# Null keys of a wide attention: their weights turned once per sequence, and who adds each head's projection to the residual

## What is computed

```
nkv = null_kv.reshape(HEADS, NUM_NULL_KV, 2, DIM_HEAD)
nk = broadcast(nkv[:, :, 0]); nv = broadcast(nkv[:, :, 1])
k = concatenate([nk, k], axis=2)
v = concatenate([nv, v], axis=2)
q = _l2norm(q) * q_scale
k = _l2norm(k) * k_scale
sim = einsum('bhid,bhjd->bhij', q, k) * ATTN_SCALE
sim = sim + dist * slopes
sim = where(causal_mask, neg, sim)
attn = softmax(sim, axis=-1)
out = einsum('bhij,bhjd->bhid', attn, v)
return out.transpose(0, 2, 1, 3).reshape(b, n, HEADS * DIM_HEAD) @ w_out
...
x = x + _L0_attn_ref(_layernorm(x, axis=-1), ...)
```

## Time and profile before

| | |
|---|---|
| Median of 3 runs | 2622.32 us (2617.93 to 2629.57) |
| Profiled execution | 2621.87 us, span of its instructions 2620.2 us |
| TensorE matmuls busy | 2392.0 us, 91% of the span |
| VectorE busy | 1722.9 us, 66% |
| ScalarE busy | 1481.1 us, 57% |
| GpSimd busy | 1605.7 us, 61% |
| Stage 0 | from the first statistics at 27.6 us to the last projection at 834 us |
| L891, additions to XR (stages 0 and 4) | 512 instructions, 376.2 us busy, 735 ns each |
| L770, products into T (stages 0 and 4) | 256 instructions, 163.8 us, 681 ns each |

### The profile page before, as it was taken

The page is one execution under the profiler, slowest core; times in us unless marked ns, Lnnn a source line. Parts: engine busy times, 40 slices in busy tenths (PEclk is TensorE's granted clock), DMA queues, the critical chain, the costliest instruction groups (busy, mean ns, idle before and its releaser), DMA issues. The chain is left out here.

```text
span 2620.2 us, 62757 instructions
## 1 busy us (share of the span) xinstructions
PE 2392.0 (91%) x24121; PEld 1873.6 (72%) x24121; DVE 1722.9 (66%) x4520; ACT 1481.1 (57%) x3071; POOL 1605.7 (61%) x2517
## 2 busy tenths in 40 slices
PE   4999999999998778888999999999999958789897
PEld 3888888888887556556777787787777748555555
DVE  4667677677775657785544467777777622477776
ACT  3666666666654457765444366666666523366665
POOL 4777777778786644443433267777777721566664
PEclk8999999999999969999999999999999979799999
DMA  3692000000000010000000000000000036000000
GB/s 115 205 331 84 2 2 2 2 2 2 2 2 1 1 53 2 2 2 1 23 1 1 3 2 6 6 4 6 6 6 4 6 116 190 17 8 10 8 4 33
DMA packets 23257, 83.12 MB, mean 32 GB/s; under 512 B 4113, under 2 KB 11026, under 8 KB 21938
## 3 DMA queue, kind: packets, MB, share of 16 engines
q1 hardware_dynamic: 19810, 71.90, 8.5%
q0 software_dynamic: 3152, 7.21, 0.9%
HBM read 71.89 MB, written 46.79 MB: 45 GB/s over the span
## 5 line engine op out<-in xcount | busy, mean ns | idle before, releaser
L891 POOL TENSOR_TENSOR XR<-XR,T 128x256 f32<-128x256 f32 x512 | 376.2, 735 | 151.9 <-DVE T L770 121.7
L645 ACT ACTIVATE P<-ps 128x384 f32<-128x384 f32 (+1 forms) x512 | 250.6, 542 | 177.4 <-PE ps L2575 176.0
L2575 PE MATMUL ps<-P,V 128*64 128x256 f32 (+3 forms) x4096 | 334.6, 348 | 7.0 <-DVE O L1396 5.2
L1380 DVE TENSOR_REDUCE bm<-ps 128x3 f32<-128x384 f32 x512 | 260.1, 550 | 100.5 <-PE ps L2575 99.8
L2575 PEld LDWEIGHTS ps<-P,V 128*64 128x64 f32 (+1 forms) x4096 | 186.3, 124 | 126.7 <-issue 32.2
L1305 ACT ACTIVATE P<-ps 128x768 f32<-128x768 f32 x256 | 207.7, 811 | 101.9 <-PE ps L2575 99.7
L781 DVE TENSOR_REDUCE sm<-ps 128x2 f32<-128x512 f32 (+1 forms) x256 | 130.8, 553 | 179.1 <-PE ps L2575 178.9
L1480 POOL TENSOR_SCALAR_AFFINE_SELECT P<-P 128x512 f32<-128x512 f32 x256 | 162.6, 635 | 124.3 <-ACT P L1305 122.4
L904 POOL TENSOR_TENSOR PS<-P 128x256 f32<-128x256 f32 x256 | 181.5, 734 | 69.5 <-ACT P L645 69.1
L2575 PE MATMUL ps<-mk,identb 128*128 128x256 bf16 (+1 forms) x1024 | 205.5, 296 | 17.2 <-DVE bm L1380 15.4
L912 POOL TENSOR_TENSOR ss<-ss,nhalf 128x16 f32<-128x16 f32 x64 | 187.8, 2934 | 5.3
(11 more groups left out here) (323 smaller groups left out, 7152.0 us busy)
## 6 DMA issues: line engine op xcount, KB each, us to landing
rows_i<-in_zero SPq DMA_DIRECT2D x16, 1208.0 KB, 32.0
rows_o<-in_zero SPq DMA_DIRECT2D x16, 1208.0 KB, 81.6
w<-in_m_w SPq DMA_DIRECT2D x23, 578.0 KB, 4.0
zt<-rows_i SPq DMA_DIRECT2D x23, 128.0 KB, 3.1
rows_o<-yo POOLq DMA_DIRECT2D x23, 128.0 KB, 3.7
stg<-in_t_w SPq DMA_DIRECT2D x11, 256.0 KB, 2.7
XR<-in_x SPq DMA_DIRECT2D x4, 512.0 KB, 8.4
out<-XR SPq DMA_DIRECT2D x8, 256.0 KB, 2.0
```

What stands on the lines that cost most here:

```text
L645: e.activation(self.P[at % 6][:, :], K.ps.ap("st", s, g, h)[:, 0:self.w], ACT.Exp, bias=0.0, scale=1.0 if kind == 0 else 0.125).then_inc(K ...
L891: p = po.e.tensor_tensor(x, x, self.T[g % 2][:, par, pr], ALU.add)
L1380: e.tensor_reduce(bm[:, h, :], K.ps.ap("mx", s, g, h)[:, 0:384].rearrange("p (a c) -> p a c", c=128), X, ALU.max, negate=True).then_inc(K. ...
L2575: return self.te.matmul(o, l, r, start=start, stop=True, skip_group_check=True)
```

## The change

Null keys: their scores are made by GpSimd (`pool_null`), the sum of the two exponents joins the sum of the others on VectorE just before the reciprocal, and GpSimd multiplies the exponents by the reciprocal into `pn` (`shared`), now [128 tokens, 64] for a whole sequence, in plain fp32 without a low part. Once per sequence a new item `null` of three steps, from tick 16b + 43, turns `pn` on TensorE, copies it on ScalarE, multiplies it by the projected null values `nvw` into a new bank `nul`, and VectorE adds that to the residual. `nvw` is made once from the null values and `wO`, in unit 0 at step 8 (`pe_nvw`, `act_nvw`). The matmuls of `pnT` leave `pe_pv`. Residual: `dve_sum` reads each 128x128 block of Y from PSUM, multiplies it by its reciprocal and adds it to XR, eight instructions a unit; `T` and GpSimd's additions are gone from stage 0. VectorE has an order of its own in which `prep` comes last in its tick. The end of a sequence (`done`) is the read of `nul`. The biases are loaded first, then the null values in one DMA in place of three. The core of the diff:

```diff
+            if kind == 0:
+                items.append((16 * b + first + 12 + unit, 2, "null", (b,), 3))
...
+        self.dve_order = [w for w in ticks(items, self.dve_rank) if not self.is_early(*w)]
...
     def done(self, b):
-        return self.summed, 4 * b + 4
+        return self.K.ps.read("nul", self.s, b) if self.kind == 0 else (self.summed, 4 * b + 4)
...
+        if name == "null":
+            return 3 if k == 0 else 2
...
+    def dve_rank(self, name, k):
+        return 6 if self.kind == 0 and name == "prep" else self.rank(name, k)
...
+    def pe_nvw(self, pe):
+        K, n = self.K, self.nvs_at
+        ps = K.ps.take(pe, self.G, "nvw")
+        K.staged(pe, n)
+        for j in range(8):
+            p = pe.e.matmul(ps[0:64, 0:128], K.stg[n % 2][:, 64 * j:64 * j + 64], K.wO[:, 128 * j:128 * j + 128],
+                            start=j == 0, stop=j == 7)
+        p.then_inc(K.ps.full_of("nvw"), 1)
+
+    def pe_null(self, pe, b, k):
+        K, s = self.K, self.s
+        if k == 0:
+            ps = K.ps.take(pe, self.G, "pnT", s, b)
+            pe.wait_ge(self.shared, 4 * b + 4)
+            K.tr(ps[0:64, 0:128], self.pn[b % 2][:, :]).then_inc(K.ps.full_of("pnT", s, b), 1)
+        if k == 1:
+            ps = K.ps.take(pe, self.G, "nul", s, b)
+            pe.wait_ge(self.nvs_in, 1)
+            pe.wait_ge(*K.ps.read("nvw"))
+            pe.wait_ge(*K.ps.read("pnT", s, b))
+            K.acc(ps[:, 0:256], self.pnT[b % 2][:, :], self.nvw[:, :], start=True).then_inc(K.ps.full_of("nul", s, b), 1)
...
-            if kind == 0:
-                pe.wait_ge(self.pnull, g + 1)
-                for i in range(2):
-                    p = K.tr(ps[0:96, 256 + 128 * i:384 + 128 * i], fv(self.pn[g % 2][:, i, :]))
...
-            for pr in range(2):
-                c = 256 * u + 128 * pr
-                K.acc(pv[:, 256 * pr:256 * pr + 256], self.nvs[:, 0, c:c + 128], self.pnT[g % 2][:, :], start=pr == 0)
-            K.acc(sm[:, 0:256], self.nvo[:, 4 * u:4 * u + 4, :].rearrange("p h c -> p (h c)"), self.pnT[g % 2][:, :],
-                  start=True)
...
+            elif name == "null":
+                if k == 2:
+                    b = a[0]
+                    xs = K.XR[:, 2 * b:2 * b + 2, :].rearrange("p t c -> p (t c)")
+                    dv.wait_ge(*K.ps.read("Y", self.s, 4 * b + 3, 1))
+                    dv.wait_ge(*K.ps.filled("nul", self.s, b))
+                    e.tensor_tensor(xs, K.ps.ap("nul", self.s, b)[:, 0:256], xs, ALU.add).then_inc(
+                        K.ps.out_of("nul", self.s, b), 1)
...
+            if kind == 0:
+                dv.after(dv.step(e.tensor_tensor(rs[:, :], sums, self.sm[g % 4][:, 48:56], ALU.add)))
+            e.reciprocal(rs[:, :], rs[:, :] if kind == 0 else sums).then_inc(K.ps.out_of("sT", s, g), 1)
...
+    def dve_sum(self, dv, b, g):
+        K, s, e, done = self.K, self.s, dv.e, [0, 0]
+        if g > 0:
+            dv.wait_ge(*K.ps.read("Y", s, g - 1, 1))
+        for par in range(2):
+            dv.wait_ge(*K.ps.filled("Y", s, g, par))
+            for pr in range(2):
+                for t in range(2):
+                    x, at = K.XR[:, 2 * b + t, :], 4 * t + 2 * pr + par
+                    if (par, pr, t) == (1, 0, 1):
+                        dv.wait_ge(*K.ps.read("Y", s, g, 0))
+                    elif par or pr:
+                        dv.after(done[t])
+                    i = e.scalar_tensor_tensor(x, K.ps.ap("Y", s, g, par)[:, 256 * pr + 128 * t:256 * pr + 128 * t + 128],
+                                               self.rs[g % 2][:, at:at + 1], x, ALU.mult, ALU.add)
+                    if pr == 1 and t == 1:
+                        i.then_inc(K.ps.out_of("Y", s, g, par), 1)
+                    else:
+                        done[t] = dv.step(i)
...
+    def pool_null(self, po, g):
...
+        po.after(po.step(e.tensor_tensor(sn, snr, rq, ALU.mult)))
+        e.tensor_tensor(sn, sn, nb, ALU.add).then_inc(self.scored, 1)
...
+            e.tensor_tensor(sm[:, 48:56], ex[:, :, 0], ex[:, :, 1], ALU.add).then_inc(self.pnull, 1)
+        if k == self.tk["out"]:
...
+            e.tensor_tensor(
+                self.pn[b % 2][:, :].rearrange("p (t h n) -> p t h n", t=2, n=2)[:, :, 4 * u:4 * u + 4, :], ex,
+                self.rs[g % 2][:, :].rearrange("p (t h) -> p t h", t=2).unsqueeze(3).to_broadcast([128, 2, 4, 2]),
+                ALU.mult).then_inc(self.shared, 1)
```

More of the change, by code:

```diff
@@ L171, in __init__ @@
         self.S = [sb(f"S{s}_{i}", [128, 256], F32) for i in range(2)]
-        self.T = [sb(f"T{s}_{i}", [128, 2, 2, 2, 128], F32) for i in range(2)]
+        if kind == 2:
+            self.T = [sb(f"T{s}_{i}", [128, 2, 2, 2, 128], F32) for i in range(2)]
         self.rs = [sb(f"rs{s}_{i}", [128, 8], F32) for i in range(2)]
@@ L182, in __init__ @@
             self.sn = [sb(f"sn{s}_{i}", [128, 64], F32) for i in range(2)]
[L183 to L186, removed]
+            self.pn = [sb(f"pn{s}_{i}", [128, 64], F32) for i in range(2)]
+            self.pnT = [sb(f"pnT{s}_{i}", [64, 128], F32) for i in range(2)]
+            self.nvw = sb(f"nvw{s}", [64, 256], F32)
             self.on = sb(f"on{s}", [128, 128], F32R)
@@ L502, in pe_pv @@
                     p = K.acc(pv[64 * par:64 * par + 64, 256 * pr + q:256 * pr + q + w], V[:, kt, 2 * pr + par, :],
[L503 removed]
+                              P[2 * pr + par][:, c:c + w], start=kt == 0 and pr == 0)
         p.then_inc(K.ps.full_of("pv", s, g), 1)
@@ L507, in pe_pv @@
                 for h in range(4):
-                    p = K.acc(sm[32 * h:32 * h + 32, q:q + w], self.one[:, 0:32], P[h][:, c:c + w])
+                    p = K.acc(sm[32 * h:32 * h + 32, q:q + w], self.one[:, 0:32], P[h][:, c:c + w], start=kt == 0)
             p.then_inc(K.ps.full_of("sm", s, g), 1)
@@ L545, in act @@
                 a[0].act(ac, a[1], k)
+            elif name == "null":
+                if k == 0:
+                    b = a[0]
+                    if b >= 2:
+                        ac.wait_ge(*self.K.ps.filled("nul", self.s, b - 2))
+                    ac.wait_ge(*self.K.ps.filled("pnT", self.s, b))
+                    ac.e.activation(self.pnT[b % 2][:, :], self.K.ps.ap("pnT", self.s, b)[0:64, 0:128], ACT.Copy).then_inc(
+                        self.K.ps.out_of("pnT", self.s, b), 1)
             elif name == "unit":
@@ L548, in act @@
                     self.act_kb(ac)
+                if self.kind == 0 and a == (0, 0) and k == 8:
+                    self.act_nvw(ac)
                 self.act_unit(ac, *a, k)
@@ L670, in dve @@
                 K.ps.out_of("beff"), 1)
-        for name, a, k in self.order:
+        for name, a, k in self.dve_order:
             if name == "prep":
@@ L820, in dve_null @@
-    def dve_null(self, dv, b, u):
-        K, s, g, e, ss, sm = self.K, self.s, 4 * b + u, dv.e, self.ss[(4 * b + u) % 4], self.sm[(4 * b + u) % 4]
-        rq = ss[:, 32:40].rearrange("p (t a r) -> p t r a", t=2, a=2).unsqueeze(4)
-        snr = self.sn[b % 2][:, :].rearrange("p (t h n) -> p t h n", t=2, n=2)[:, :, 4 * u:4 * u + 4, :].rearrange(
-            "p t (a r) n -> p t r a n", a=2)
-        sn = sm[:, 16:32].rearrange("p (t r a n) -> p t r a n", t=2, r=2, a=2)
-        nb = K.pc("nbias", 8 * u, 8).rearrange("p (a r n) -> p r a n", a=2, r=2)
-        dv.wait_ge(*K.ps.read("sn", s, b))
-        dv.wait_ge(self.unitq, 2 * g + 1)
-        if g >= 4:
-            dv.wait_ge(self.rec, g - 3)
-        for t in range(2):
-            d = dv.step(e.tensor_tensor(sn[:, t], snr[:, t], rq[:, t].to_broadcast([128, 2, 2, 2]), ALU.mult))
-        dv.after(d)
-        for t in range(2):
-            d = dv.step(e.tensor_tensor(sn[:, t], sn[:, t], nb, ALU.add))
-        dv.after(d)
+    def dve_null(self, dv, b, u):
+        g, e, sm = 4 * b + u, dv.e, self.sm[(4 * b + u) % 4]
+        dv.wait_ge(self.scored, g + 1)
@@ L867, in pool @@
                     self.pool_halves(po, 4 * a[0] + a[1], k - 1 - self.tk["st"])
-                if k == self.tk["out"] + (1 if self.kind == 2 else 0):
+                if self.kind == 2 and k == self.tk["out"] + 1:
                     self.pool_sum(po, *a)
@@ L935, in sp @@
         if self.kind == 0:
-            for n, (a, b) in enumerate(((0, 512), (512, 1024), (1024, 1040))):
-                n += self.nvs_at
-                K.sp_stage(sp, n, K.stg[n % 2][0:96, 0:b - a], K.t["nvs"][:, a:b])
             for c in range(5):
```

107 lines of the change are left out of this document (55 added, 52 removed).

## The result

The changed kernel takes 2641.54 us, the median of five runs (2637.66 to 2645.2), against 2622.32 before. The ratio is 1.0071, 95% interval 1.005 to 1.0092: slower by 19 us where 8 were forecast, inside the range. By the forecast's own bands (faster under 2609, slower over 2635) that is "slower", which had 0.38, and not "no change", which had 0.45. Its profiled execution took 2645.2 us, span 2643.5.

The account below looks back on a forecast made before the run. TensorE was taken to bound the first wide attention. Removed 51.4 us, added 59.7 (three bank waits included), net +8.3 on the profiled 2621.87 gave 2630.2, rounded up to 2631; range 2603 to 2660.

Parts of the forecast that it names:

- TensorE's matmuls and transposes: TensorE, each unit: two pn transposes and three pnT matmuls removed, 0.76 us, 48.6 us over 64 units.
- null transpose and product: TensorE, once per sequence: one added transpose and one fp32 matmul of 256 columns, 0.61 us, 9.8 us over 16.
- KL, tick 2: Unit with the next sequence's z and statistics: TensorE waits 1.35 us for KL's bank, 14 times, 18.9 us.
- bank of zT, tick 6: VectorE takes prep last, so v waits 0.60 us for the bank zT's low half frees, 14 times, 8.4 us.
- bank of nul, tick 14: Scores opening tick 14 wait for VectorE's null addition, behind two maxima and a reduction: 1.44 us, 15 times, 21.6 us.
- The sum step: VectorE, each unit: eight 128x128 steps, 0.26 us each, 2.08 in all, where T held 1.20.
- the first rival: VectorE's eight sum steps stand end to end, 0.34 us each, 2.72 in all: 2657 us; chance 0.16.
- second rival: The new TensorE waits bring clock falls to 0.50, ten times 1.5 us: 2646 us; chance 0.12.
- The end of the stage: Stage 1 waits for the last residual, which comes earlier without GpSimd's adds: gain 1.4 us.
- The case of the three waits: The forecast itself, with TensorE's waits for the KL, zT and nul banks: 2618 to 2642 us; chance 0.50.
- The regular unit's room of 0.11 us: Regular units: KL's bank is usable at 5.56 us, TensorE arrives at 5.67, so no wait.
- The rival "TensorE stays the bound": Bank waits lie elsewhere or VectorE is further ahead, so only TensorE's sum counts: 2581 us; chance 0.12.

Follow-up runs that it names:

- the kernel with the old residual: The changed kernel with T on VectorE and GpSimd's four additions back in stage 0, null keys as changed: 2664.86 us, ratio 1.0173 to the kernel before.
- the run: The changed kernel with GpSimd's early statistics for stage 1 (`ahead`) last in their tick: 2630.94 us, ratio 1.0045 to the kernel before.
- four ordering edits: The changed kernel with null addition first, early statistics last, z behind KL, and prep last except zT's low half: 2585.01 us, ratio 0.9863 to the kernel before.

## Why the prediction was right or wrong

The mechanism was right: TensorE's saving counts in full only where nothing is late, and three banks come back late once a sequence, at the three places and behind the three steps named. Each was taken away by itself and its price came back. The sizes, per sequence:

| Term, us per sequence | predicted | timeline after | by removing it |
|---|---|---|---|
| TensorE's matmuls and transposes | -3.04 | -2.36 | |
| its waits for pn | -0.10 | -0.10 | |
| null transpose and product | +0.61 | +0.83 | |
| KL, tick 2 | +1.35 | +1.13 | 1.14 |
| bank of zT, tick 6 | +0.60 | +0.37 | 0.41 |
| bank of nul, tick 14 | +1.44 | +1.39 | 1.33 |
| sum | +0.86 | +1.26 | drift +1.17 |

**The step that failed: the saving, 0.76 us a unit.** It was read as the distances of starts of the removed steps, 0.21 + 0.33 + 0.22. What stands in front of `P,V` changed too: 0.36 us from `raw` to `pnT,nvs` before, 0.53 from `raw` to `P,V` after. So 0.59 us is saved, and 64 x 0.17 = 10.9 us are missing. This also makes TensorE arrive later at the banks of KL and zT, and both waits are shorter than predicted. At zT's it arrives 4.84 us after R (508.26) in place of 4.69, and goes on 5.21 after R in place of 5.29. At KL's it arrives 5.84 after R (495.98 to 501.70, and 0.12) in place of 5.75. That is only 0.09 later, because the 5.75 had in it the 0.09 us by which KL held TensorE already. It goes on 6.98 after R in place of 7.10. So VectorE's side was right to 0.1 us in both.

**The null product.** 0.50 us was taken from `P,V`; the records give 527.65 - 526.81 - 0.12 = 0.72 us, where 0.12 is the pace of `wA,zT`. Its transpose lengthens the way from `nm` to `P,V` from 0.75 to 0.86 (522.31 to 523.17). Together 0.83: the product just above its upper bound of 0.7, and 3.5 us more over 16 sequences.

**The sum step was right.** 0.26 us a step and 2.06 in all, where 2.08 was forecast and 2.72 was the first rival's. The group of VectorE by shape, 0 to 830 us:

```profile
L849 DVE SCALAR_TENSOR_TENSOR XR<-ps,rs,XR 128x128 f32<-128x128 f32 x480 | 129.1, 343 | 0.0
...
L730 DVE TENSOR_TENSOR XR<-ps,XR 128x256 f32<-128x256 f32 x14 | 5.8, 415 | 0.0
```

One is 343 ns long and they start 0.26 apart, each waiting for the one before the last. By the rule of the Trainium skill (VectorE: DVE Perf Modes, "The DRAIN you can't avoid") they would stand end to end; this trace does not agree. The same section allows that an instruction which is not held starts earlier.

**The clock, second rival.** It did not come as priced. Through the 1.39 us at the null bank the granted clock stayed at full, the 2.4 GHz level:

```profile
530.00:532.00 2.00, 0.98 (x8) 0.74 (x7) 2.00 (x4) 1.32 (x3) 0.00 (x0) 1.00 0.00 0
532.00:534.00 2.00, 1.80 (x26) 1.59 (x28) 0.37 (x3) 0.10 (x1) 0.22 (x1) 1.00 0.00 0
```

It fell during the 4.18 us for `pn`, and, in the kernel with the old residual, during the 1.91 us for `raw`. The Trainium skill (TensorE: Matmul & The Clock Gate, "Part 1: The HAM clock gate") says that an idle TensorE is throttled back; both falls agree. The waits of 1.0 to 1.4 us, and 6 of the 14 waits of 1.9 us for `raw`, show that not every idle stretch brings one.

**What was missed: `pn` behind `ahead`.** The prediction went through VectorE's queue and the PSUM ring, and of GpSimd it said only that it gets "two small steps per unit" and, with ScalarE's, that "Neither is on the path". But `shared` is a new step on GpSimd that TensorE waits for. Its rank puts it behind the early statistics, once in the stage. Worth 6.0 us by the run. The kernel before had a gap of its own at this place, on its TensorE:

```profile
767.20 0.63 PE L2578 MATMUL ps<-ident,raw 128*128 128x128 f32 x4 [1.17 <-POOL raw L917]
...
768.59 0.47 PE L2578 MATMUL ps<-ident,pn 128*96 128x128 f32 x2 [0.54 <-POOL pn L928]
```

With it went a stretch of 3.4 us at half clock (768.8 to 772.2, part of it in the earlier trace rows), which costs half of that. So the net is 6.0 - (1.17 + 0.54 + 1.7) = 2.6 us.

**The end of the stage** gained 0.6 us, not 1.4: the time from the last `wO,OT` to the first statistics went from 6.47 us (833.27 to 839.74) to 5.92 (852.25 to 858.17), and VectorE's last addition starts at 855.73, 2 us ahead of a cast at 857.83 that waits for ScalarE and stands in front of those statistics. So the residual does not set that start.

The account over the stage: -64 x 0.59 - 1.4 + 16 x 0.83 + 14 x 1.13 + 14 x 0.37 + 15 x 1.39 + 2.6 - 0.6 = +18.0 us. Measured +18.4. The start of the stage is not in this sum. The one-time projection of the null values, put at 1 us in a start where TensorE was said to wait anyway, does not lie in that wait but behind it: 2.74 us from its start to the next matmul (47.58 to 50.32, changed kernel, most of it at half clock). What it costs in the end is not shown, since unit 7 comes only 0.76 us later than before, and runs differ by more than that there. So the agreement to 0.4 us is closer than the parts allow.

**How much of the number was luck.** 17.8 us were missing from the forecast (10.9 of the saving, 3.5 of the null product, 2.6 at `pn`, 0.8 at the end), and 7.1 too much was in it (3.1 for KL, 3.2 for zT, 0.8 for the null bank), so the errors cancel in part. The case of the three waits was given 2618 to 2642, and 2641.54 lies in it by half a microsecond.

**Not as the prediction said it would show.** The wait for the null bank is called "issue", not `<-DVE XR`. By the forecast's own test ("wrong if TensorE shows no waits for XR") I would have dropped a right theory; the gap in the starts of `mk,identb` was the row to name. GpSimd's busy time fell by 167 us (170 forecast). The drift makes the period 49.6 us where "about 49" was said. The regular unit's room of 0.11 us held: no wait shows there.

**The rival "TensorE stays the bound"** gave 2581, and with the three waits taken away by order alone the kernel takes 2585: the change holds about that much. The match is in part luck. The rival counts 48.6 us of removed work where 37.8 are there, and the run has, against the kernel before, 3.96 us less between units 59 and 63, where the gap near 767 us is gone, and 2.5 us less at the end of the stage.

## What to carry to other kernels

When an engine that bounds a kernel gets less to do, look first at which of its buffers were returned just in time; here one bank had no room before the change, and half of a saving of 2.36 us a sequence was lost there with nothing else altered. A new or moved reader of a ring buffer belongs where the ring comes round to it, not where it is convenient: four ordering edits without any change of work were worth 2.1%, some 55 us, nearly three times what the change cost. And price what is taken out from the distance between its two neighbours, not from the steps themselves, since the neighbours' own distance changes.

## What was unexpected of the hardware

- `P,V` starts 0.53 us after four fp32 transposes of `raw`, while the 96-row matmuls of `pnT` started 0.36 after them; with these gone, 0.17 of their 0.55 us stays. What inside the engine sets this was not looked into.
- An fp32 product of 64 rows and 256 columns, two instructions, takes 0.63 us between its start and the next (527.02 to 527.65), more than the 0.50 that `P,V` has for as many columns.
- A wait for a PSUM bank that VectorE frees late can appear in the profile without a releaser, as idle time of "issue".
- One and the same wait of 1.9 us of TensorE, once a sequence in the kernel with the old residual, was followed or met by a fall of the granted clock to 0.50 in 8 of 14 sequences and not in the other 6.
